# Reordering SyncE's queue around the context's round trip, and moving two normalisations from VectorE to GpSimd

## The reference

```python
h = _layernorm(x) * (1 + ca) + sa                      # modulated input
# inside the attention block
x1 = (h - mu) * rsqrt(var + eps) * ln1_g + ln1_b       # "norm 1" (xn in the kernel)
Q = x1 @ q_U @ q_V + q_b ;  K, V alike                 # 16 heads of 8
attn = softmax(causal(Q K^T * scale)); ctx = attn @ V
h = h + ctx @ out_U @ out_V + out_b
x2 = (h - mu) * rsqrt(var + eps) * ln2_g + ln2_b       # "norm 2" (after_n in the kernel)
out = h + gelu(x2 @ fc1_U @ fc1_V + fc1_b) @ fc2_U @ fc2_V + fc2_b
x = x + ga * out
```

## Time and profile before

| what | value |
|---|---|
| median of 3 runs | 699.83 us (698.48 to 700.15) |
| the profiled execution's own time | 706.22 us |
| its span | 704.5 us, mean granted PE clock 0.959 |
| busy shares | PE 86%, DVE 64%, ACT 58%, POOL 43% |
| attention's steps | about 69 us to 382 us of the span |

### The profile page before, as it was taken

How to read it: one execution, slowest core, us unless ns; L and a number is a source line. 1 busy time by engine, 2 the same in 40 slices (tenths; PEclk the granted TensorE clock), 3 DMA queues, 4 the chain that set the end, 5 groups by cost and what they waited for, 6 DMA issues and landing times.

```text
span 704.5 us, 16609 instructions
## 1 busy us (share of the span) xinstructions
PE 607.5 (86%) x5841; PEld 401.2 (57%) x5841; DVE 450.2 (64%) x1346; ACT 408.1 (58%) x718; POOL 301.2 (43%) x478
## 2 busy tenths in 40 slices
PE   3988888887888879778868977999897999999997
PEld 2643444443444434334324666766765999999993
DVE  5759888888899857767732878777673222222227
ACT  0432678687677758656658465676434555555550
POOL 4232334253443605232313438666671445545452
PEclk9999799999999989998989988999899999999999
DMA  9653142443343424340463411211236788878779
GB/s 196 196 168 87 57 131 101 141 140 111 120 154 121 148 84 153 118 133 28 146 178 112 131 44 55 81 51 49 66 94 189 216 226 222 240 224 226 230 217 316
DMA packets 85842, 100.40 MB, mean 143 GB/s; under 512 B 13808, under 2 KB 67736, under 8 KB 85664
## 3 DMA queue, kind: packets, MB, share of 16 engines
q1 hardware_dynamic: 76608, 86.53, 41.1%
q0 software_dynamic: 4544, 9.45, 3.7%
q10 hardware_dynamic: 4608, 3.35, 1.9%
HBM read 59.89 MB, written 37.31 MB: 138 GB/s over the span
## 4 chain that ended last, share of the span: by engine, by line
PE 46%; DMA 13%; DVE 12%; SPq 9%; issue 9%; ACT 6%; POOL 5%; POOLq 0%; ACTq 0%; DVEq 0%
PE ps_r L1543 7%; PE ps_s L1533 7%; PE ps_pv L1351 6%; DVE row_max L1735 6%; PE ps_pv L1429 4%; DMA arena<-slots_d 3%; PE ps_r L1289 3%; POOL slots_d L931 3%; PE ps_r L1294 3%; DMA k_d<-arena_early 2%; DMA arena<-y_d 2%; PE ps_s L1334 2%; SPq L612 2%; PE ps_s L1437 2%; SPq L609 2%
## 5 line engine op out<-in xcount | busy, mean ns | idle before, releaser
L1735 DVE TENSOR_REDUCE row_max<-ps_r 128x1 f32<-128x384 f32 (+3 forms) x384 | 211.4, 594 | 45.8 <-PE ps_r L1294 43.1
L1007 ACT ACTIVATE arena<-ps_s 128x1024 f32<-128x1024 f32 (+1 forms) x192 | 168.6, 882 | 86.8 <-PE ps_s L1334 85.1
L977 POOL DMA_INDIRECT y_d<-arena,target x78 | 74.9, 960 | 86.5 <-DVE arena L1942 74.3
L1351 PE MATMUL ps_pv<-arena 128*32 128x512 f32 (+3 forms) x1024 | 95.4, 471 | 0.0
L1289 PEld LDWEIGHTS ps_r<-ident_h,later_q 64*128 64x128 bf16 x768 | 24.7, 94 | 121.3 <-DVE row_max L1735 78.9
L1289 PE MATMUL ps_r<-ident_h,later_q 64*128 64x64 bf16 (+1 forms) x768 | 49.5, 206 | 42.7 <-DVE row_max L1735 42.3
L1938 DVE TENSOR_TENSOR arena<-ps_r,arena_early 128x256 f32<-128x256 f32 x39 | 16.6, 425 | 108.2 <-PE ps_r L1543 108.2
L931 POOL DMA_INDIRECT slots_d<-arena,slots x64 | 65.3, 1020 | 18.2 <-issue 18.2
L1294 PE MATMUL ps_r<-arena 48*128 48x384 bf16 (+3 forms) x512 | 70.8, 310 | 0.0
L1334 PE MATMUL ps_s<-arena 51*128 51x256 bf16 (+3 forms) x512 | 70.6, 310 | 0.0
L1543 PEld LDWEIGHTS ps_r<-arena 128*128 128x128 f32 x480 | 58.2, 192 | 1.5
(11 more groups left out here) (240 smaller groups left out, 1129.0 us busy)
## 6 DMA issues: line engine op xcount, KB each, us to landing
arena<-in_ew SPq DMA_DIRECT2D x30, 514.0 KB
ctx_d<-ctx_raw SPq DMA_DIRECT2D x32, 256.0 KB, 2.6
arena<-q_d SPq DMA_DIRECT2D x64, 96.0 KB, 2.7
arena<-k_d SPq DMA_DIRECT2D x64, 96.0 KB, 2.7
arena<-slots_d SPq DMA_DIRECT2D x39, 132.0 KB, 3.0
arena_early<-in_ew SPq DMA_DIRECT2D x9, 514.0 KB, 3.8
arena<-y_d SPq DMA_DIRECT2D x8, 512.0 KB, 6.8
q_d<-arena_early SPq DMA_DIRECT2D x8, 384.0 KB, 2.5
```

The lines of the kernel that those rows point to most:

```text
L977: pool.indirect_dma_start(y_d[:], bass.IndirectOffsetOnAxis(ap=target[:, k, c:c + 1], axis=0), res[:, k, c, :], None).then_inc(put[k], 16)
L1007: act.activation(dst, src, ACT.Exp, scale=SCALE).then_inc(exp_done, 1)
L1351: mm = pe.matmul(ps_pv[32 * j:32 * j + 32, kt * P:S], v_sb[b % 2][:, kt, GROUPS * j + g, :], probs[:, p % 2, at:at + length], start=(kt == ...
L1735: dve.reduce_max(row_max[:, m % 2, js[0] % 2, j:j + len(js), i], src, AXIS.X).then_inc(max_taken, 1)
```

## The change

SP's queue is put in another order: the context's store first, then the sums (offset 6), then, one step later than before (offset 7), the reciprocals' reload and the context's four loads; then the store of the maxima, the reciprocals' store, the K stores, the stack loads (now one group a step, offsets -6 to -3), the load of the maxima, and the Q stores last. DVE's reciprocal stands behind unit 5 rather than 10. Both normalisings go from DVE to POOL, behind `split_max` (for norm 1 only those made inside the steps; the first three batches stay on DVE). POOL's output bias moves from offset 3 to 2.

```diff
-NORM_EARLY = 3
+NORM_EARLY, BIAS_AT = 3, 2
@@ SyncE
+                    def load_sums(b):
                         for k in range(2):
                             wait(sp, ctx_stored[k], 32 * (b + 1))
                         wait(sp, rec_ready, b)
+                        sp.dma_start(sums[:], ...).then_inc(sum_loaded, 16)
+                    def store_rec(b):
+                        wait(sp, rec_ready, b + 1)
+                        wait(sp, rec_loaded, 16 * b)
+                        sp.dma_start(rec_d..., recs[:]).then_inc(rec_stored, 16)
+                    def load_rec_and_ctx(b):
+                        wait(sp, ctx_ready, b)
+                        wait(sp, rec_stored, 16 * (b + 1))
+                        sp.dma_start(rec_rows[:], ...).then_inc(rec_loaded, 16)
                         for j in range(JH):
                             sp.dma_start(ctx_t[...], cells[0:DH, j]...).then_inc(ctx_loaded, 16)
                     def step(n):
-                        for g, later in ((0, 0), (1, 0), (2, 1), (3, 2)):
-                            ... load_stack(b, g, ...)
+                        if 0 <= n - 2 < NG:
+                            store_ctx(n - 2)
                         if batch_at(n, CTX_AT) is not None:
-                            load_ctx(batch_at(n, CTX_AT))
+                            load_sums(batch_at(n, CTX_AT))
+                        if batch_at(n, CTX_AT + 1) is not None:
+                            load_rec_and_ctx(batch_at(n, CTX_AT + 1))
                         if 0 <= n + LAG - 1 < NG:
                             store_max(n + LAG - 1)
-                        if batch_at(n, K_OUT_AT - 1) is not None:
-                            store_stack(batch_at(n, K_OUT_AT - 1), 0)
+                        if batch_at(n, CTX_AT) is not None:
+                            store_rec(batch_at(n, CTX_AT))
                         if batch_at(n, K_OUT_AT) is not None:
                             store_stack(batch_at(n, K_OUT_AT), 1)
...
-                        if 0 <= n - 2 < NG:
-                            store_ctx(n - 2)
+                        for g in range(GROUPS):
+                            b = batch_at(n, LOAD_AT + g)
+                            ... load_stack(b, g, ...)
                         if 0 <= n + LAG - 1 < NG:
                             load_max(n + LAG - 1)
-                        if batch_at(n, CTX_AT) is not None:
-                            move_rec(batch_at(n, CTX_AT))
+                        if batch_at(n, K_OUT_AT - 1) is not None:
+                            store_stack(batch_at(n, K_OUT_AT - 1), 0)
@@ GpSimd
+                    def normalise(b):
+                        pool.wait_ge(h_rstd, b + 1)
+                        wait(pool, filled["T"], b - 1)
+                        for i in range(NT):
+                            pool.tensor_scalar(xn[:, b % 2, i, :], h_sb[:, NT * b + i, :], moments[:, 1, b % 2, i, 0:1],
+                                               rstd[:, 1, b % 2, i:i + 1], ALU.subtract, ALU.mult).then_inc(xn_ready, 1)
+                    def normalise_after(b):
+                        ... the same, from after_rstd, into after_n
                     def step(n):
                         if 0 <= n + LAG - 1 < NG:
                             split_max(n + LAG - 1)
+                        if norm_at(n, NORM_AT) is not None:
+                            normalise(norm_at(n, NORM_AT))
+                        if batch_at(n, AFTER_NORM_AT) is not None:
+                            normalise_after(batch_at(n, AFTER_NORM_AT))
...
-                        b = batch_at(n, 3)
+                        b = batch_at(n, BIAS_AT)
@@ VectorE: both normalisings removed from layer_norm, and
-                            if u == 10 and batch_at(n, CTX_AT) is not None:
+                            if u == 5 and batch_at(n, CTX_AT) is not None:
```

More of the change, by code:

```diff
@@ L638, in store_ctx @@
                         sp.dma_start(ctx_d[b % 2, :, g], ctx_raw[:, p % 2, :]).then_inc(ctx_stored[p % 2], 16)
-                    def load_ctx(b):
+                    def load_sums(b):
                         for k in range(2):
@@ L644, in load_ctx @@
                         wait(sp, rec_ready, b)
+                        sums_d = ctx_d[b % 2].rearrange("(j r) g s -> r j g s", j=JH)[DH].rearrange("j g s -> j (g s)")
+                        sp.dma_start(sums[:], sums_d.rearrange("j (c s) -> j c s", s=HEADS * S // P)).then_inc(sum_loaded, 16)
+                    def store_rec(b):
+                        wait(sp, rec_ready, b + 1)
+                        wait(sp, rec_loaded, 16 * b)
+                        sp.dma_start(rec_d.rearrange("h (c s) -> (h c) s", s=HEADS * S // P), recs[:]).then_inc(rec_stored, 16)
+                    def load_rec_and_ctx(b):
+                        wait(sp, ctx_ready, b)
+                        wait(sp, rec_stored, 16 * (b + 1))
+                        sp.dma_start(rec_rows[:], rec_d.unsqueeze(1).to_broadcast([HEADS, DH, S])).then_inc(rec_loaded, 16)
                         cells = ctx_d[b % 2].rearrange("(j r) g s -> r j g s", j=JH)
-                        sp.dma_start(sums[:], cells[DH].rearrange("j g s -> j (g s)").rearrange("j (c s) -> j c s", s=HEADS * S // P)).then_inc(sum_loaded, 16)
-                        wait(sp, ctx_ready, b)
                         for j in range(JH):
@@ L675, in step @@
                                 load_stack(0, 0, "q")
-                        if 0 <= n - 2 < NG:
-                            store_ctx(n - 2)
+                        for g in range(GROUPS):
+                            b = batch_at(n, LOAD_AT + g)
+                            if b is not None:
+                                load_stack(b, g, "k" if b == 0 and g == 0 else "qk")
                         if 0 <= n + LAG - 1 < NG:
                             load_max(n + LAG - 1)
-                        if batch_at(n, CTX_AT) is not None:
-                            move_rec(batch_at(n, CTX_AT))
+                        if batch_at(n, K_OUT_AT - 1) is not None:
+                            store_stack(batch_at(n, K_OUT_AT - 1), 0)
                         if batch_at(n, AFTER_OUT_AT) is not None:
@@ L844, in qk_lowest @@
                         pool.tensor_tensor(qk_part[:, m, 2], qk_rest[:, m], qk_part[:, m, 1], ALU.subtract).then_inc(qk_low, 1)
+                    def normalise(b):
[5 more added lines that the diff above has]
+                    def normalise_after(b):
+                        pool.wait_ge(after_rstd, b + 1)
+                        wait(pool, filled["U"], b)
+                        for i in range(NT):
+                            pool.tensor_scalar(after_n[:, i, :], h_sb[:, NT * b + i, :], moments[:, 2, b % 2, i, 0:1],
+                                               rstd[:, 2, b % 2, i:i + 1], ALU.subtract, ALU.mult).then_inc(after_ready, 1)
                     def split_max(m):
@@ L1599, in stats_after @@
                         stats_of(2, h_sb, b, i, after_stats)
[L1601 to L1606, removed]
                     def stats_all_x(b):
@@ L1711, in layer_norm @@
                                     stats_h(b, i)
-                        b = norm_at(n, NORM_AT)
-                        if b is not None:
-                            normalise(b, quarters[0] // 2 + 2 * second)
                         b = batch_at(n, AFTER_STATS_AT)
@@ L1721, in layer_norm @@
                                     stats_after(b, i)
[L1722 to L1725, removed]
                     def take_max(m, u):
```

10 lines of the change are left out of this document (removed).

## The result

The changed kernel took 711.37 us in the median of four runs (710.15 to 713.43) against 699.99 us for the kernel before beside it: a ratio of 1.0152 (95% interval 1.0114 to 1.0189). That is slower, as the whole interval lies above 1, and outside the forecast range. Of the rivals, the one that ended on the other side (the wait at unit 5 takes the place of the one at unit 10) came true in its mechanism; it had 704.8 us, 6.6 us too few.

What follows compares the result with a forecast made beforehand. Most attention stretches were taken as bound by PE and its hand-overs, others by stalls. 14.5 + 0.8 - 3.0 - 0.8 = 11.5 us off 699.8 gives 688.3, stated as 688.5 us; range 683.5 to 699 us.

Steps and rivals of the forecast that it cites:

- the wait at unit 5 takes the place of the one at unit 10: Rival, steps 6 to 22: sums 2 to 3 us late, clock falls, 19.5 us lost, 704.8 us, slower; chance 0.14.
- the price of DVE's wait at unit 5: Steps 6, 10, 14, 18 and 22: waiting for the sums costs 0.6 us each, 3.0 us in all.
- 15.3 gross: Attention: gain before costs, 14.5 us of removed stalls plus 0.8 us from less work on DVE.
- The length of that wait: DVE before the reciprocal, worked out in step 14: sums usable at 211.7 us, a wait of some 1.2 us.
- POOL's normalise: Normalises on POOL: about 0.48 us each, four 1.9 us; the K store about 0.3 us late.
- The removed stalls: Stretches 10, 16, 18 and 22 to 24: late sums and late split of the maxima go, 14.5 us off.
- DVE's relief: Stretches 9, 13 and 17: 1.1 us less DVE work is worth 0.25 us each, 0.8 us off.
- Norm 2 behind the attention's end: Step 34, where PE waits for norm 2: 1.11 us on DVE become 1.9 on POOL, 0.8 us lost.
- The port: Rival: POOL's bias or norms meet DVE's modulation instructions, 1.3 us lost in four steps, 5 us back, 693.5 us; chance 0.07.

Runs made afterwards that it cites:

- the early sums: Changed kernel with the sums' load issued one step earlier, right behind the maxima's store, ahead of K stores and loads; reciprocal at unit 5: 0.9791 of the kernel before.
- the kernel with these shorter waits: Changed kernel with POOL's first normalise placed behind the lowest part of K, reciprocal still at unit 5: 1.0086 of the kernel before.

## Why the prediction was wrong, step by step

- **The step that failed is the price of DVE's wait at unit 5: 0.6 us for each of five steps, 3.0 us.** With the wait at the 1.0 to 1.4 us that it assumed, the five stretches took 2.3, 4.0, 3.7, 3.7 and 3.8 us more than with the early sums, 17.4 us together and nearly six times the term. With the longer waits of the changed kernel it is 25.0 us, and the ratios say the same: 1.0152 - 0.9791, of 700 us, is 25.3. The prediction wrote that "PE has a little slack" there. It had seen the clock fall in stretches 10, 18 and 24 and kept that price for a wait of 2 to 3 us, in its rival; the runs show it behind 0.56 us of DVE's wait and 1.09 of PE's. By itself this turns the forecast, 17.4 us against 15.3 gross; the kernel with these shorter waits was slower too (1.0086).
- **The length of that wait was short as well**: 2.4 to 3.2 us where 1.2 was said. In step 14 POOL held the K store for 1.4 us (0.3 in the prediction), and the landing took 219.55 - 216.74 = 2.8 us where 2.43 was taken: 1.5 us more, and 1.2 + 1.5 are the 2.7 us of the row. With the hold gone, the queue ran as worked out: from the maxima's store to the usable sums it took 8.4 us (205.84 to 214.26), where the prediction had 8.65.
- **POOL's normalise** takes 0.78 us and not 0.48. The interpolation between rows of 16 and 512 columns put a one-input instruction with two scalars from tiles too near its lower row. The 1.16 us of `qk_lowest` stood behind it on POOL, and the prediction said so; it gave it 0.3 us because SP's own queue seemed to cover it.
- **The removed stalls, 14.5 us**: right in place and about right in size. Stretches 16 and 24 fell in the changed kernel; the others only once the wait was away. With the early sums, stretches 10, 16, 18 and 22 to 24 are 16.9 us shorter than in the first profile and the attention 18.1 us, but that profile is of an execution 6.4 us over its median; by the ratio the whole gain is 14.6 us, against the 14.5 that the forecast has without its wait (15.3 - 0.8). So close an agreement is partly luck, as the terms are off both ways. The attribution of the stalls was half right: the order alone, with the reciprocal at unit 10, moved them to steps 12, 16, 20 and 24.
- **DVE's relief, 0.8 us**: stretches 9, 13 and 17 fell by 0.24, 0.29 and 0.23 us, as said. Missed were the 0.5 us in stretches 10 and 14, which showed only without the wait (8.48 us with the normalises on POOL, 8.98 and 8.99 on DVE).
- **Norm 2 behind the attention's end, 0.8 us**: undersized with the normalise. PE's transposes of step 34 start 11.5 us behind the last context copy, where it was 9.35: 2.2 us later.
- **The port**: stretches 7, 11 and 15 of the changed kernel took 10.54, 11.34 and 10.07 us where they took 9.55, 9.59 and 9.58 with the early sums, 3.2 us together. The late sums bring `ctx_n` and the bias on POOL beside DVE's shifts of the modulation, whose slowest one took 1.41 us (0.97 with the early sums, 0.35 in the middle); in stretch 11 PE waits 1.18 us for DVE behind it. That this is all of the 3.2 us is argued and not shown.
- **The range and the chances.** The upper end, 699.0 us, stood below the slower rival, which had 0.14. That rival was to decide "at some 3.9 us lost per batch"; this is the rival's own cost (19.5 us over five), and the point at which the cost eats the gain is lower, (15.3 - 0.8) / 5 = 2.9 us. So even less would have turned the sign than the prediction told its reader. Measured are 25.0 / 5 = 5.0 us. A time like the forecast's is one that these parts can reach, with another place for the sums' load: 685 us.

## What to carry to other kernels

Price a new wait on a queue that feeds PE by what the same trace shows behind any short stall, clock included, and not by its own length: here 1.1 us of wait cost 3.7 us. Where a consumer is moved forward, move its load forward by as much in the issuing engine's queue, to a place ahead of whatever waits for a slower engine; with both, the changed kernel was 2% faster than the one before, and the earlier reciprocal alone made that one 3% slower. When several parts of a change feed one another, work out each alone as well: the three that were run alone here (the reciprocal, the order, the normalises) were each a loss alone, and all are in the fastest kernel.

## What the runs showed of the hardware that was not expected

- PE's standing for 1.41 and 1.09 us (0.88 and 0.56 us of wait on DVE) was followed by a granted clock of 0.50, the level of 1.2 GHz, in steps 10 and 14 of the kernel with the normalises on DVE, and so was its standing for 1.5 to 1.9 us in all five steps of the one with the first normalise behind K; with 0.92 us of wait, and PE standing 1.46, in step 22 of the former the clock stayed at 1.00. The low level lasted 6 to 10 us and made the 118 matmul records of stretches 10 and 14 take 10.1 to 11.4 us instead of 7.4.
- A subtract and multiply with two scalars per partition on 128x128 floats takes 792 ns on POOL, where DVE takes 339. This is by the median of 20 instructions on POOL and of 32 on DVE.
- A DVE instruction with two inputs in SBUF that starts 0.02 us behind a POOL bias took 1.41 us instead of 0.34, while DVE's reductions out of PSUM beside POOL's work kept their 1.29 us for two. The Trainium skill ("SBUF — State Buffer", section "SBUF: two separate sides") has it that whichever of the two starts first keeps the shared pair for its whole instruction; by that rule the trace agrees, as 1.28 us of the bias and a part of DVE's own time make the 1.41.
